# Causal convolution as pairs of 32x32 blocks of TensorE's array, with channels in another order

## The reference

```
xr = h @ in_proj_w.T                      # 256 -> 1024
xs, res = split(xr)                       # 512 channels each
xc = conv1d(xs, conv_w, groups=512, taps=4, causal) + conv_b   # every channel by itself
xs = silu(xc)
dt, B, C = split(xs @ x_proj_w.T)
delta = softplus(dt @ dt_proj_w.T + dt_proj_b)
h_t = exp(delta*A) * h_{t-1} + delta*xs*B     # 16 states for each of 512 channels
y = sum over states(h_t * C) * silu(res);  x = x + ga * (y @ out_proj_w.T)
```

## Time and profile before

| | |
|---|---|
| median of 3 runs | 2515.86 us |
| span of the profiled execution | 2510.4 us, so 5.5 us less than the median run |
| its own time outside the span | not recorded; taken as those 5.5 us |
| PE (matmul) busy | 2181.1 us, 87% |
| DVE busy | 1929.5 us, 77% |
| POOL busy | 1955.0 us, 78% |
| ACT busy | 1390.4 us, 55% |

### The profile page before, as it was taken

How to read it: one execution, slowest core, us unless ns; L and a number is a source line. 1 busy time by engine, 2 the same in 40 slices (tenths; PEclk the granted TensorE clock), 3 DMA queues, 4 the chain that set the end, 5 groups by cost and what they waited for, 6 DMA issues and landing times. The chain is left out here.

```text
span 2510.4 us, 31164 instructions
## 1 busy us (share of the span) xinstructions
PE 2181.1 (87%) x7664; PEld 1059.5 (42%) x7665; DVE 1929.5 (77%) x2060; ACT 1390.4 (55%) x2472; POOL 1955.0 (78%) x840
## 2 busy tenths in 40 slices
PE   8769998989989898999898988989857649999997
PEld 3214343443434343444343443434323335556654
DVE  2799899999999999989899999999897162222222
ACT  3666666667575766666666667576644232222221
POOL 1999889898989898989889898989897014555553
PEclk9878889898989898988989898989878869999999
DMA  5443242424232323434242424232321062222221
GB/s 155 129 112 96 73 102 66 100 71 112 79 94 73 97 76 95 107 85 102 73 102 67 101 69 114 80 92 77 91 68 39 26 208 77 85 84 82 87 85 45
DMA packets 149402, 224.40 MB, mean 89 GB/s; under 512 B 48227, under 2 KB 85617, under 8 KB 145138
## 3 DMA queue, kind: packets, MB, share of 16 engines
q1 hardware_dynamic: 135858, 182.44, 27.8%
q0 software_dynamic: 13376, 40.12, 5.1%
HBM read 99.48 MB, written 31.47 MB: 52 GB/s over the span
## 5 line engine op out<-in xcount | busy, mean ns | idle before, releaser
L1029 POOL TENSOR_TENSOR hs<-hs,c_rep 128x2048 f32<-128x2048 f32 x256 | 1154.8, 4532 | 41.3 <-ACT state L772 41.1
L869 DVE TENSOR_TENSOR_SCAN hs<-dA,state,hs 128x512 f32<-128x512 f32 x768 | 931.4, 1265 | 20.7 <-ACT dA L752 16.4
L752 ACT ACTIVATE dA<-d_rep,a 128x512 f32<-128x512 f32 x1024 | 688.8, 686 | 411.2 <-DVE hs L869 409.2
L1022 POOL TENSOR_TENSOR hs<-u_rep,b_rep 128x2048 f32<-128x2048 f32 x96 | 435.8, 4540 | 88.6 <-PE bank L516 88.5
L856 DVE TENSOR_TENSOR hs<-u_ps,b_rep 128x2048 f32<-128x2048 f32 x160 | 361.2, 2274 | 10.1 <-issue 5.1
L487 PE MATMUL bank<-n,w1s 128*128 128x512 f32 x512 | 269.0, 663 | 68.0 <-DVE delta L837 39.2
L869 DVE TENSOR_TENSOR_SCAN hs<-dA,hs 128x512 f32<-128x512 f32 x256 | 294.2, 1204 | 20.0 <-ACT dA L752 18.8
L516 PE MATMUL bank<-hs,spread 128*32 128x512 f32 x2048 | 280.4, 696 | 31.1 <-POOL hs L1029 27.0
L1414 DVE TENSOR_TENSOR hid<-z,sg 128x512 f32<-128x512 f32 x70 | 48.4, 692 | 298.2 <-ACT sg L1392 298.2
L1332 PE MATMUL z<-w1r,hT 128*128 x560 | 260.6, 608 | 3.5 <-issue 2.4
L445 PE MATMUL bank<-xin,w_in 128*128 128x512 f32 x512 | 246.3, 621 | 7.9 <-ACT xin L599 7.9
(11 more groups left out here) (174 smaller groups left out, 2566.3 us busy)
## 6 DMA issues: line engine op xcount, KB each, us to landing
d_rep<-delta SPq DMA_DIRECT2D x1024, 64.0 KB, 2.0
u_rep<-us SPq DMA_DIRECT2D x384, 64.0 KB, 2.0
b_rep<-bc_rows SPq DMA_DIRECT2D x64, 256.0 KB, 4.4
c_rep<-bc_rows SPq DMA_DIRECT2D x64, 256.0 KB, 7.8
xres<-in_x SPq DMA_DIRECT2D x16, 512.0 KB, 3.3
token_rows<-xpad SPq DMA_DIRECT2D x32, 256.0 KB, 2.4
token_rows<-xres SPq DMA_DIRECT2D x16, 512.0 KB, 2.9
xin<-in_x SPq DMA_DIRECT2D x15, 512.0 KB, 9.4
```

The source lines that it names most:

```text
L752: nc.scalar.activation(dA[:, u % ABANK, :], d_rep[:, q, :], ACT.Exp, scale=t["a"][:, u:u + 1]).then_inc(da_ready, 1)
L869: nc.vector.tensor_tensor_scan(hs[:, s % RING, g, :], dA[:, u % ABANK, :], hs[:, s % RING, g, :], state[:, u:u + 1] if m else 0.0, ALU.mul ...
L1022: nc.gpsimd.tensor_tensor(hs[:, s % RING], u_rep[:, i % UBUF, :].unsqueeze(1).to_broadcast([P, NG, T]), b_rep[:, par, :].rearrange("p (g t ...
L1029: nc.gpsimd.tensor_tensor(hs[:, s % RING, :, :], hs[:, s % RING, :, :], c_rep[:, par, :].rearrange("p (g t) -> p g t", g=NG), ALU.mult).th ...
```

## The change

The convolution is computed in blocks of 32 channels. For the pair (0, 1) the matmuls of block rows 0 and 1 of all four channel tiles are issued, for the pair (2, 3) those of block rows 2 and 3. Each matmul has 32 rows and 32 columns at the array position (32 r, 32 b): it reads partitions 32 r to 32 r + 31 of channel tile b, and writes partitions 32 b to 32 b + 31 of the bank of r. So a bank then holds one block of each channel tile, and the order of the channels in `us`, and behind it, differs; the weights are permuted on the host to fit. Both banks of a pair are taken before its first matmul, all four tiles of `xpad` are waited for, and CV 1 and CV 3 do nothing where they stand. `conv_made` is still raised once for each bank, at the end.

```diff
-                elif kind == "CV":
-                    pe.wait_ge(xs_ready, KI * f + j + 1)
-                    for k in range(KCONV):
-                        last = nc.tensor.matmul(ps_[:, :], t["w_conv"][:, j, k, :], xpad[:, j, k:k + T], start=(k == 0), stop=(k == KCONV - 1))
+            def convolve(j, c, f):
+                if j % 2:
+                    return
+                first = take_bank(pe, ("CV", j), c, f)
+                pe.sem_inc(held, 1)
+                second = take_bank(pe, ("CV", j + 1), c, f)
+                pe.sem_inc(held, 1)
+                pair = ((j, first), (j + 1, second))
+                hold(pe, xs_ready, KI * f + KI, held)
+                for k in range(KCONV):
+                    for b in range(KI):
+                        for r, ps_ in pair:
+                            rows = slice(DS * r, DS * r + DS)
+                            last = nc.tensor.matmul(ps_[DS * b:DS * b + DS, :], t["w_conv"][rows, b, k, :], xpad[rows, b, k:k + T],
+                                                    start=(k == 0), stop=(k == KCONV - 1), skip_group_check=True, tile_position=(DS * r, DS * b))
+                            if k == KCONV - 1 and b == KI - 1:
+                                last.then_inc(conv_made, 1)
...
-                    last = nc.vector.tensor_scalar(t["w_conv"][:, j, k, :], t["ident"][:], cw[:, j, k:k + 1], None, ALU.mult)
+                    last = nc.vector.tensor_scalar(t["w_conv"][:, j, k, :], t["gather"], cw[:, j, k:k + 1], None, ALU.mult)
...
+    held_by = np.arange(DI).reshape(SPC, KI, DS).transpose(1, 0, 2).reshape(DI)
...
-        "w_out": c(a["L0_attn_out_proj_w"].T), "wg": c(a["L0_ffn_Wg_DN"]), "w1": c(a["L0_ffn_Wl1_ND2H"]), "w2": c(a["L0_ffn_Wl2_NHD"]),
+        "w_out": c(a["L0_attn_out_proj_w"].T[held_by]), "wg": c(a["L0_ffn_Wg_DN"]), "w1": c(a["L0_ffn_Wl1_ND2H"]), "w2": c(a["L0_ffn_Wl2_NHD"]),
```

More of the change, by code:

```diff
@@ L434, in group @@
                     return sum_states(g, f, c)
+                if kind == "CV":
+                    return convolve(j, c, f)
                 ps_ = take_bank(pe, g, c, f)
@@ L1437, in build @@
                 "w_in": sb("w_in", [P, KD, 2 * DI]), "w_x": sb("w_x", [P, KI, PROJ]), "w_dt": sb("w_dt", [DT_ROWS, DI]),
-                "w_out": sb("w_out", [P, KI, D]), "w_conv": sb("w_conv", [P, KI, KCONV, P]), "sa": sb("sa", [P, KD, BATCH]),
+                "w_out": sb("w_out", [P, KI, D]), "w_conv": sb("w_conv", [P, KI, KCONV, DS]), "sa": sb("sa", [P, KD, BATCH]),
                 "ca": sb("ca", [P, KD, BATCH]), "sb2": sb("sb2", [P, KD, BATCH]), "cb2": sb("cb2", [P, KD, BATCH]),
@@ L1455, in laid_out @@
     c = np.ascontiguousarray
+    held_by = np.arange(DI).reshape(SPC, KI, DS).transpose(1, 0, 2).reshape(DI)
+    w_in = a["L0_attn_in_proj_w"].T
     return {
         "x": c(a["L0_attn_x"].reshape(BATCH * SEQ, D)),
[L1459 to L1463, removed]
-        "w_out": c(a["L0_attn_out_proj_w"].T), "wg": c(a["L0_ffn_Wg_DN"]), "w1": c(a["L0_ffn_Wl1_ND2H"]), "w2": c(a["L0_ffn_Wl2_NHD"]),
+        "w_in": c(np.concatenate([w_in[:, :DI], w_in[:, DI + held_by]], axis=1)), "conv_w": c(a["L0_attn_conv_w"].reshape(KI, P, KCONV).transpose(1, 0, 2)),
+        "conv_b": c(a["L0_attn_conv_b"][held_by].reshape(KI, P).T),
+        "w_x": c(np.insert(a["L0_attn_x_proj_w"].T[held_by], DT_RANK, 0.0, axis=1)),
+        "w_dt": c(np.concatenate([a["L0_attn_dt_proj_w"].T, a["L0_attn_dt_proj_b"][None]])[:, held_by]),
+        "a_cols": c(a["L0_attn_A_log"][held_by].reshape(KI, SPC, DS, NF, NG).transpose(3, 2, 0, 1, 4).reshape(P, NSET * NG)),
+        "w_out": c(a["L0_attn_out_proj_w"].T[held_by]), "wg": c(a["L0_ffn_Wg_DN"]), "w1": c(a["L0_ffn_Wl1_ND2H"]), "w2": c(a["L0_ffn_Wl2_NHD"]),
         "c": c(a["L0_c"].reshape(BATCH, KD, P).transpose(2, 1, 0)), "wmod": c(a["L0_wmod"]),
```

## The result

The changed kernel takes 2556.41 us (median of 4 runs, 2552.67 to 2558.07) against 2515.59 (2515.13 to 2516.01) for the kernel before on the same chip: ratio 1.0166, 95% interval 1.0154 to 1.0178. It is slower by 41 us; forecast was 2552.4. The profiled execution has a span of 2555.0 us, 44.6 more than before.

A forecast was written before the change was run, and what follows sets the result against it. DVE was taken to set the pace between sets 3 and 8, its scans above all. 15 x (0.4 + 2.3) = 40.5 us, less 4, gives +36.5: span 2546.9, plus 5.5 outside it, 2552.4 us; range 2511 to 2585.

The forecast's parts named there:

- Eight at once: Convolution pairs on PE: eight of the 64 instructions run at once, so a pair takes 8 steps, 3.64 us.
- The second rival: Convolution pairs: eight don't run at once, a pair takes 7.28 us; about 2614 us, or 2579 with clock up; chance 0.12.
- Nothing in the loop waits for the first pair: First pair in the loop: PE's shorter time buys nothing directly, as OP 0 behind it needs DVE's gate product.
- The wait on CV 1's reading reaches ACT, then DVE, with 0.4 us at full clock: Second pair waits for CV 1 to be read; ACT stands before CV 2, DVE late by 0.4 us a chunk, bounds 0 to 0.8.
- The clock, 2.3 us a chunk: Second pair, behind PE's idle time, runs partly at 1.2 GHz: 2.3 us a chunk, bounds 0 to 3.64.
- No room in the rest of the chunk: Behind set 5: the delay goes to DVE whole and isn't won back, as DVE has no wait until set 10.
- START, -4 us: START: L566 and XP behind the convolutions start 4.1 us sooner; 4 us gained, bounds 0 to 4.1.
- The sum: Whole kernel: 15 x (0.4 + 2.3) = 40.5 us, less 4: +36.5, span 2546.9, with 5.5 outside the span 2552.4 us.
- faster: Rival at SUM 1: PE comes to set 9 at full clock, 15 x 1.57 = 24 us go, time 2488; chance 0.08.

The follow-up runs named there:

- the stall away: Changed kernel with ACT's reading of CV 1 moved from set 4 to set 3, directly behind CV 0: 2511.48 us, ratio 0.9985.
- the wait alone: Kernel before, full-size convolution, with one wait added in the loop: CV 2 also waits until ACT has read CV 1. 2542.48 us, ratio 1.0099.
- PE kept busy: Changed kernel, in the loop first pair's matmuls issued twice and four matmuls of constants before the second pair: 2534.45 us, ratio 1.0074.
- The fill in START: Changed kernel with CV 1 read at set 3, plus matmuls of constants in START, one before the first pair, two before the second: 2507.38 us.
- set 8 filled: Changed kernel with CV 1 read at set 3, plus three matmuls of constants at set 8, before DT 0 and DT 1: 2482.53 us.
- the same fill: Kernel before with the same three matmuls of constants at set 8: 2486.43 us, ratio 0.9892.
- the same at set 11: Two matmuls of constants before DT 3, added to changed kernel with early read, START and set 8 fills: 2473.59 us; to kernel before with set 8 fill: 2489.66.

## Why the prediction was right, and where it was off

- *Eight at once*: right. 3.66 us for 64 instructions, at the price of SUM's row. The second rival (pairs of 7.28 us) falls.
- *Nothing in the loop waits for the first pair*: right. With the stall away the kernel is at 0.9985, and DVE's scans of set 5 start as before.
- *The wait on CV 1's reading reaches ACT, then DVE, with 0.4 us at full clock*: right in place and size. The cleanest rows are the chunks in which the clock held: 0.45 us at the first scan of set 5 with the wait alone, and 0.46 to 0.66 us with PE kept busy (at the scan behind the table loads, in nine chunks).
- *The clock, 2.3 us a chunk*: right in size: wait and clock together cost 43.5 us in the 15 chunks that convolve (4.7 in chunk 0, 38.8 in the others), 2.9 us each against 2.7. The way there was drawn wrong, so that the size is so near is in part luck. I had OP 0 at full clock and 5.0 us of idle time behind it. The clock fell in the 2.9 us in front of OP 0, OP 0 took 6.62 us, and only 1.9 us of idle time were left before the second pair. By then the clock was back, and it fell again within the pair, which paid all the same. So each idle stretch was followed by a fall of its own, and the first stretch is made by the part of the change that I had priced at nothing.
- *No room in the rest of the chunk*: nearly right. The first scan behind the table loads is late by 3.1 us on the average of 14 chunks, the chunk by 2.8.
- *START, -4 us*: this term failed. I let the second pair run at full clock, with 1.5 us of idle time in front of it, though the sum for the loop assumed the opposite for the same situation. It took 7.08 us, and the first scan came 1.4 us later than before instead of 4 us sooner: 5.4 us off, the largest miss in the sum. The fill in START gave 4.1 us back (2511.48 to 2507.38, measured apart; 2.8 us at the first scan).
- The sum: 15 x 2.7 - 4 = 36.5 forecast; by the trace 1.4 + 4.7 + 38.8 and little else, 44.6; by the medians 41. The span is 8.1 us above the forecast of 2546.9, the median only 4.0 above that of 2552.4. The difference is the 5.5 us that I had added for the time outside the span: in the changed kernel's profiled run it is 1.9 us (2556.89 against 2555.0). That half of the miss cancels is luck.
- The rival *faster* named the right place: the low clock ahead of SUM 1 is worth 29 us (set 8 filled, 2511.48 to 2482.53, measured apart). Its 24 us were priced otherwise, by SUM 1's own 1.57 us in each chunk; SUM 1 got only 0.55 us shorter on the mean, and started 2.2 us sooner, so that the two numbers are near each other is luck. And the change doesn't touch it, and the same fill gives as much on the kernel before.

## What to carry to other kernels

Making an engine faster between two waits only makes it idle, and here TensorE paid for idle time with its clock, in what came next. Before speeding up a stage, find who waits for it; before joining two steps into one, look which reader stands in the queue between their waits, and move that reader (here one table entry) in the same change. Where TensorE has idle places of one to three microseconds ahead of a result that others wait for, a few matmuls of constants there can be worth more than a faster algorithm: 29 us against none here. It has to be tried at each place: the same at set 11 only moved the idle time.

## What the runs showed of the hardware that I had not expected

- A third kind of overlap: matmuls of the next row group, into another bank, start before the previous group's are through, without being interleaved in the program. 64 instructions of two banks took 5.4 us, where four at once would take 7.3. In the chunk shown (from 315.29) the second bank's first four start at 317.06, while the last three steps of the first bank, which stand before them in the program, start at 317.46 to 318.34. So "strictly in the written order", as the kernel before is described, doesn't hold of TensorE's matmuls here.
- The clock also fell under a TensorE that wasn't idle. Narrow matmuls of one row group ran without a gap, and the granted clock was 1.00 from 433 to 436 us and 0.80 from 436 to 439, with the spread behind them at half speed.
- The Trainium skill (TensorE: Matmul & The Clock Gate, Part 3) gives a spacing of about 4 ns between the starts of packed matmuls. Here eight instructions of a step and its whole latency fit into one row of 0.66 us, where one by itself takes 0.61 (the median of L511):

```profile
323.60 0.66 PE L511 MATMUL bank<-xpad,w_conv 32*32 32x512 f32 x8
```

That leaves some 7 ns for each of the seven that follow the first, and so the trace agrees with the rule in kind, at nearly twice the figure.
